# The beginning of a first attention: x of the first batch normalised and turned between two parts of a hidden layer, keys ahead of the other batches' statistics

## The chip, the cores and the metric

The kernel runs on one core of one Trainium2 chip. The metric is the device time of one execution in microseconds; the time of a kernel is the median of its runs. Engine names are those of the profile: PE (TensorE), DVE (VectorE), ACT (ScalarE), POOL (GpSimd), SP (SyncE, which issues the DMAs).

## The reference, cut to what matters

The whole program is two layers, each of an attention with a bias, a second attention, a mixture of experts and a feed-forward block, on x of shape (4, 512, 256). The change touches the first attention's beginning alone. What that attention computes, cut:

```python
xn = ln(x, g_norm)                                # 4 x 512 rows of 256
q = heads(xn @ Wq)                                # 16 heads of 64
k, v = split(xn @ Wkv)                            # one head of 64 for all
k = concatenate([null_kv[0], k]); v = concatenate([null_kv[1], v])
q = l2norm(q) * q_scale;  k = l2norm(k) * k_scale
# the bias: a small network over the positions, one table for all batches
h = silu(ln(pos @ w0 + b0, g0))
h = silu(ln(h @ w1 + b1, g1))                     # the hidden layer
bias = (h @ w2 + b2)[i - j]                       # 16 heads
sim = q k^T * 8 + bias, causal and key mask
out = ln(softmax(sim) v @ Wout, g_out)
```

## The kernel before, in words

`cond_attention` holds five programs, one for each engine, written out in order by hand. An engine takes its instructions in that order and waits on semaphores; `link` makes DVE wait for its own last result. PSUM has eight banks. Banks 0 to 3 hold the small network's results, banks 4 to 7 are a ring (`Ring`): each product of PE takes the next of them with `ring.put`, and waits there until the product four places before it has been emptied by DVE or ACT.

The small network has 640 positions in `NP` = 5 tiles of 128 rows and 256 columns. DVE makes the first hidden rows, ACT applies Silu (`hidden_units`), PE turns them (`turn_hidden`), DVE and ACT copy one half each out of PSUM (`move_hidden`), PE multiplies them by `w1` tile by tile (`hidden_layer`), DVE adds `b1` and takes statistics (`hidden_sums`), aggregates them and adds a constant (`hidden_root`, the TENSOR_SCALAR at L726), ACT takes the Sqrt, DVE normalises (`hidden_rows`), ACT applies Silu, and PE turns the rows again and makes the table (`table`). DVE adds `b2` and SP stores the table to memory and loads it back eight times in its banded form (`cb_toep`), which POOL adds to the masks (L957).

Beside that runs the first batch: four tiles of x, statistics by `row_statistics(0, NT, ...)`, `normalise_x` (L568), `turn_x` on PE into two ring banks (L295), emptied by DVE (bank of c = 0, L573) and ACT (c = 1, L1059), then eight blocks of queries (`queries(0, m)`, PE L329; ACT squares and copies each block, L976 and L977), keys and values (L304), sums of the squared queries over heads (`query_squares`, L337), scores with the null key (`null_scores`, L319), turned keys (L312). DVE normalises the keys (`keys_values`, `scaled_keys`). The null key itself is normalised by `null_key_square`, a Sqrt on ACT and `null_key`; POOL then makes two products of it with Wq (L196), which DVE adds up (`key_sums`, L202). `row_statistics(NT, B * NT, ...)` takes the statistics of the other three batches' x, twelve tiles (L752, L755, L757), which are first used when batch 1 is normalised within the loop of the attention.

The orders before are: PE: turn_hidden(0), the whole hidden layer, both x turns, queries 0, turn_hidden(1), queries 1, table, queries 2 and 3, keys and values, squares, queries 4 to 7, null scores. DVE and ACT: as the left side of the diff shows. The loads are issued by SP in one list at the start (`sync_program`, L1113).

Of the kernel before, what the change touches and what calls it, by code (L numbers as in the profile page):

```python
# [28 lines left out]
NT = S // P  # L29
# [206 lines left out]
def cond_attention(nc, env, w, layer, later=None, gated=None):  # L236
# [8 lines left out]
    with ExitStack() as ctx:  # L245
# [44 lines left out]
        def tensor_program(pe):  # L290
# [144 lines left out]
            def hidden_layer():  # L435
                pe.wait_ge(sm["rp_w"], 16 * 2)
                pe.wait_ge(sm["rp_ev"], 1)
                pe.wait_ge(sm["rp_ev2"], 1)
                for t in range(NP):
# [26 lines left out]
            if L0:  # L466
                turn_hidden(0)
                hidden_layer()
                turn_x(0, 0)
                turn_x(0, 1)  # L470
                pe.wait_ge(sm["cw_q"], 16 * 2)
                queries(0, 0)
                turn_hidden(1)
                queries(0, 1)
                table()
                queries(0, 2)
# [85 lines left out]
        def vector_program(dve):  # L562
# [210 lines left out]
            if L0:  # L773
# [10 lines left out]
                row_statistics(0, NT, "xs_first")  # L784
                null_key_square()
                move_hidden(0)
# [3 lines left out]
                dve.wait_ge(sm["xs_std"], 1)  # L790
                link(dve.reciprocal(rstd[:, 0:NT], r["xve"][:, 0:NT]))
                normalise_x(0)
# [4 lines left out]
                dve.wait_ge(sm["cw_q"], 16 * 2)  # L797
                turn_x(0, 0)
# [8 lines left out]
                dve.tensor_scalar(r["tab"][:, 512:NPOS], PS[0:H, 1, 0:NPOS - 512], r["b2"], None, ALU.add).then_inc(sm["rp_out"], 1)  # L807
                row_statistics(NT, B * NT, "xs_in")
# [3 lines left out]
                keys_values(0)  # L812
                scaled_keys(0)
                query_squares(0, 0)
                dve.wait_ge(sm["xs_std"], 2)
                link(dve.reciprocal(rstd[:, NT:], r["xve"][:, NT:]))
# [8 lines left out]
                spread(("bc", 0, 1), ("q", 0, 1), 0, 1)  # L825
            else:
# [142 lines left out]
        def scalar_program(act):  # L969
# [78 lines left out]
            if L0:  # L1048
                hidden_root(0)
                hidden_units(0)  # L1050
                move_hidden(0)
                act.wait_ge(sm["xs_var"], 1)
                act.activation(r["xve"][:, 0:NT], r["xve"][:, 0:NT], ACT.Sqrt).then_inc(sm["xs_std"], 1)
                act.wait_ge(sm["cw_sum"], 1)
                act.activation(w["sc"][:, 2:3], w["sc"][:, 1:2], ACT.Sqrt).then_inc(sm["cw_root"], 1)
                hidden_root(1)
                bank = ring.take(act, ("x", 0, 1))
                act.wait_ge(sm["cw_q"], 16 * 2)
                act.activation(xnT(0, 1), PS[:, bank, :], ACT.Copy, scale=w["g_in"][:, 1:2]).then_inc(ring.emptied(("x", 0, 1)), 1)  # L1059
                hidden_units(1)  # L1060
                queries(0, 0)
                move_hidden(1)
                for m in range(1, SET + 1):
                    queries(0, m)
                key_root(0)
# [2665 lines left out]
```

## Time and profile before

| | |
|---|---|
| median of 3 runs | 2887.36 us (2885.25 to 2887.46) |
| profiled execution | 2888.08 us, span 2886.3 us |
| PE, weight loads, DVE, ACT, POOL busy | 93%, 55%, 50%, 36%, 32% of the span |
| mean granted clock of PE | 0.96 |
| instructions | 36961 |

The span is the time between the first and the last instruction of the profiled execution; the device time has a little around it. A busy engine is not the same as an engine that sets the end: PE is busy most of the span, and the question in each stretch is what it waits for when it is not. A row of the timeline has the start in us from the span's start, how long the merged instructions took together, the engine, the line of the kernel, the operation, output and inputs with their shapes, the count, and in brackets how long the engine had stood idle before and what released it. The granted clock is 1.00 at PE's full 2.4 GHz and 0.50 at 1.2 GHz.

### The profile page before, as it was taken

Reading aid. Unit: us, or ns where it says so; the run is one execution under the profiler, and the core shown is the slowest. Engines: PE = TensorE matmul, PEld = TensorE weight load, DVE = VectorE, ACT = ScalarE, POOL = GpSimd, SP = SyncE. Lnnn points to the kernel's source line nnn. Section 1 sums busy time; section 2 is a strip of 40 time slices with the busy share of each in tenths; the row PEclk is TensorE's granted clock in tenths of the full one; section 3 lists DMA queues with packets and bytes.
Section 4 is the critical chain, followed back from the end, with each engine's and each line's share of the span. In section 5 each row is a group of like instructions: output and inputs, shape, how many; then the busy total and the mean of one; then the engine's idle time right before and its main releaser. Section 6 shows DMA issues by size and latency. Waiting matters only on the chain. (4 is left out here: it accounts for less than half of the span.)

```text
span 2886.3 us, 36961 instructions
## 1 busy us (share of the span) xinstructions
PE 2680.2 (93%) x13448; PEld 1575.0 (55%) x13448; DVE 1430.9 (50%) x3211; ACT 1052.6 (36%) x2439; POOL 923.5 (32%) x962
## 2 busy tenths in 40 slices
PE   6999998889999889999999999799999899899987
PEld 3555655433333246847748658555555566445555
DVE  6465564356666343234233233655655478355543
ACT  3667675044444201111111111265666255112211
POOL 3555454167676521202102001475655100000000
PEclk9999999799999889999999999999999899899996
DMA  4000001000000060000000010332333000400000
GB/s 147 1 1 1 1 1 19 1 1 1 1 1 1 1 219 1 1 0 1 0 0 1 0 39 1 98 114 89 109 97 103 1 1 1 135 1 15 15 23 22
DMA packets 87961, 91.37 MB, mean 32 GB/s; under 512 B 20982, under 2 KB 71551, under 8 KB 87656
## 3 DMA queue, kind: packets, MB, share of 16 engines
q1 hardware_dynamic: 87784, 89.02, 9.8%
q8 instruction: 110, 1.80, 0.3%
q14 instruction: 67, 0.55, 0.1%
HBM read 86.86 MB, written 2.14 MB: 31 GB/s over the span
## 5 line engine op out<-in xcount | busy, mean ns | idle before, releaser
L957 POOL TENSOR_TENSOR cb_sc<-cb_toep,cb_mk 128x128 f32<-128x128 f32 (+3 forms) x256 | 215.5, 870 | 214.4 <-ACT cb_pr L999 203.8
L957 POOL TENSOR_TENSOR cb_bias<-cb_bias,cb_mk 128x128 f32<-128x128 f32 (+3 forms) x256 | 213.8, 865 | 163.3 <-DMA cb_bias<-in_fside_16xSxS 163.3
L390 PE MATMUL PS<-ident,cb_pr 128*128 128x128 f32 x1280 | 198.9, 287 | 29.3 <-ACT cb_pr L999 27.7
L1542 DVE TENSOR_REDUCE gb_bmax<-PS 128x16 f32<-128x1024 f32 x128 | 156.4, 1223 | 128.5 <-PE PS L1353 127.5
L390 PEld LDWEIGHTS PS<-ident,cb_pr 128*128 128x128 f32 x1280 | 138.6, 143 | 122.3 <-issue 111.4
L661 DVE CUSTOM_DVE_ANT_0 cb_sc<-PS,cb_sc,cb_sneg 128x128 f32<-128x128 f32 (+3 forms) x256 | 130.6, 557 | 138.5 <-PE PS L379 137.0
L3100 POOL TENSOR_TENSOR eb_S<-ff_h 128x1024 f32<-128x1024 f32 x16 | 37.7, 2355 | 466.8 <-PE PS L2054 466.7
L1353 PE MATMUL PS<-gb_ks,gb_qs 32*128 32x512 f32 x512 | 145.9, 647 | 34.1 <-DVE gb_bmax L1542 26.5
L1006 ACT ACTIVATE cb_pt<-PS 128x128 f32<-128x128 f32 (+3 forms) x448 | 162.4, 409 | 36.6 <-PE PS L390 36.1
L1679 ACT ACTIVATE gb_pt<-PS 128x1024 f32<-128x1024 f32 x128 | 130.7, 1021 | 121.1 <-PE PS L1359 112.2
L661 DVE CUSTOM_DVE_ANT_0 cb_bias<-PS,cb_bias,cb_sneg 128x128 f32<-128x128 f32 (+3 forms) x256 | 129.4, 548 | 91.0 <-PE PS L379 90.0
L2054 PE MATMUL PS<-eb_g,ff_h 128*128 128x256 f32 x768 | 173.6, 379 | 0.0
L402 PE MATMUL PS<-cb_pt,cb_kv 128*64 128x512 f32 (+3 forms) x1024 | 157.7, 451 | 10.8 <-DVE cb_pt L669 8.0
L1742 POOL TENSOR_TENSOR gb_pa<-gb_pa,gb_pt 128x512 f32<-128x512 f32 x128 | 159.7, 1273 | 10.9 <-ACT gb_pt L1679 10.6
L379 PE MATMUL PS<-cb_kT,cb_QT 64*128 64x128 f32 (+3 forms) x768 | 156.6, 485 | 1.3 <-DVE cb_kT L602 0.9
L2054 PEld LDWEIGHTS PS<-eb_g,ff_h 128*128 128x128 f32 x768 | 145.9, 190 | 21.5 <-issue 1.9
L999 ACT ACTIVATE cb_pr<-cb_bias,cb_nm 128x128 f32<-128x128 f32 (+3 forms) x256 | 141.4, 557 | 38.6 <-DVE cb_nm L661 38.3
L1359 PE MATMUL PS<-gb_qs,gb_ks 32*128 32x512 f32 x512 | 149.6, 649 | 2.9 <-ACT gb_pt L1679 2.8
L999 ACT ACTIVATE cb_pr<-cb_sc,cb_nm 128x128 f32<-128x128 f32 (+3 forms) x256 | 141.6, 559 | 22.0 <-DVE cb_nm L661 20.6
L402 PEld LDWEIGHTS PS<-cb_pt,cb_kv 128*64 128x64 f32 x1024 | 76.2, 140 | 113.4 <-issue 99.2
L1742 POOL TENSOR_TENSOR gb_pa<-gb_pt 128x512 f32<-128x512 f32 x64 | 79.8, 1269 | 121.8 <-ACT gb_pt L1679 121.8
L2017 PE MATMUL PS<-eb_yT,ff_w 128*128 128x512 f32 x256 | 111.3, 593 | 0.7 <-issue 0.7
(522 smaller groups left out, 5110.9 us busy)
## 6 DMA issues: line engine op xcount, KB each, us to landing
cb_bias<-in_fside_16xSxS SPq DMA_DIRECT2D x64, 256.0 KB, 2.8
cb_bias<-in_fside_16xSxS SPq DMA_DIRECT2D x64, 192.0 KB, 2.4
ff_h<-in_L_ffn_h_w SPq DMA_DIRECT2D x2, 4096.0 KB, 22.7
cb_bias<-in_fside_16xSxS SPq DMA_DIRECT2D x64, 128.0 KB, 2.2
cb_toep<-rel_table SPq DMA_DIRECT2D x8, 512.0 KB, 8.8
cb_bias<-in_fside_16xSxS SPq DMA_DIRECT2D x64, 64.0 KB, 2.3
eb_M<-in_L_ffn_attention_mask SPq DMA_DIRECT2D x4, 1024.0 KB, 5.3
ff_w<-in_L_ffn_w_w SPq DMA_DIRECT2D x3, 1024.0 KB, 7.8
```

What stands on the lines that cost most here:

```text
L379: ins = pe.matmul(PS[:, 2 * (v % 2) + e, 0:n], QT[b % 2][part, m, t * P:t * P + P], kT[part, b % 2, 0:n], start=True, stop=True, tile_posi ...
L390: ins = pe.transpose(PS[:, bank, j * P:j * P + P], pr[:, v % 2, e, j * P:j * P + P], ident)
L402: ins = pe.matmul(PS[part, bank, j * P:S], kv[:, b % 2, j, DH:2 * DH], pt[:, e, j, j * P:S], start=(j == 0), stop=(j == NT - 1), tile_posi ...
L661: ins = dve.tensor_tensor_reduce(out=biases(v, e), in0=PS[:, 2 * (v % 2) + e, 0:n], in1=biases(v, e), scale=-1.0, scalar=sneg[:, b % 2, t, ...
L957: ins = pool.tensor_tensor(biases(v, e), turned(h, n) if L0 else biases(v, e), mk[:, b % 2, packed(t):packed(t) + n], ALU.add)
L999: ins = act.activation(pr[:, v % 2, e, 0:n], biases(v, e), ACT.Exp, bias=nm[:, b % 2, t, k:k + 1], scale=-1.0, accum_out=rs[:, b % 2, t, k ...
L1006: act.activation(pt[:, e, 0:t + 1, t * P:t * P + P], PS[:, bank, 0:width(t)].rearrange("p (j k) -> p j k", k=P), ACT.Copy).then_inc(ring.e ...
L1353: ins = pe.matmul(PS[:, first_bank(x) + e, :], qs[rows(g), n % 3, t * P:t * P + P], ks[rows(g), n % 3, :], start=True, stop=True, tile_pos ...
L1359: ins = pe.matmul(PS[:, 2 + e, :], ks[rows(g), n % 3, t * P:t * P + P], qs[rows(g), n % 3, :], start=True, stop=True, tile_position=(32 * ...
L1542: dve.tensor_reduce(bmax[:, n % 2, t, g:g + 2, 0:NB], PS[:, bank:bank + 2, :].rearrange("p g (n k) -> p g n k", k=64), AX.X, ALU.max)\
L1742: pool.tensor_tensor(pa[:, n % 2, h, :], before, pt[:, n % 2, h, t, :], ALU.add).then_inc(sm["gt_pc"], 1)
L2054: ins = pe.matmul(PS[:, bank, m * HS:m * HS + HS], lhs[:, k, m * P:m * P + P], rhs[:, k, :], start=(m == k == 0), stop=(m == 1 and k == KH ...
```

## The change

Only orders are changed; no instruction is added and none is left out.

On PE the hidden layer is cut: tiles 0 and 1, then both x turns, then tiles 2 to 4. Two blocks of queries come ahead of turn_hidden(1), block 2 ahead of the table, block 3 behind it.

On DVE `move_hidden(0)`, the reciprocal and `normalise_x(0)` come ahead of `null_key_square` and of the first two tiles' sums, and the copy of the turned x comes ahead of `null_key` and the other sums. After the table, the keys, the copy of the squares and the scaled keys come ahead of the twelve tiles' statistics; the reciprocal of those statistics goes to the end, behind the first two spreads.

On ACT the Sqrt of the first batch's variances comes ahead of `move_hidden(0)`, the copy of the turned x ahead of the second hidden root, two blocks of queries ahead of `move_hidden(1)`, the key root after block 3, and the Sqrt of the twelve tiles' variances after block 7.

```diff
-            def hidden_layer():
-                pe.wait_ge(sm["rp_w"], 16 * 2)
-                pe.wait_ge(sm["rp_ev"], 1)
-                pe.wait_ge(sm["rp_ev2"], 1)
-                for t in range(NP):
+            def hidden_layer(tiles):
+                for t in tiles:
+                    if t == 0:
+                        pe.wait_ge(sm["rp_w"], 16 * 2)
+                        pe.wait_ge(sm["rp_ev"], 1)
+                        pe.wait_ge(sm["rp_ev2"], 1)
...
 (PE)
                 turn_hidden(0)
-                hidden_layer()
+                hidden_layer((0, 1))
                 turn_x(0, 0)
                 turn_x(0, 1)
+                hidden_layer((2, 3, 4))
                 pe.wait_ge(sm["cw_q"], 16 * 2)
                 queries(0, 0)
+                queries(0, 1)
                 turn_hidden(1)
-                queries(0, 1)
+                queries(0, 2)
                 table()
-                queries(0, 2)
                 queries(0, 3)
 (DVE)
                 row_statistics(0, NT, "xs_first")
+                move_hidden(0)
+                dve.wait_ge(sm["xs_std"], 1)
+                link(dve.reciprocal(rstd[:, 0:NT], r["xve"][:, 0:NT]))
+                normalise_x(0)
                 null_key_square()
-                move_hidden(0)
                 dve.wait_ge(sm["rp_w"], 16 * 2)
                 hidden_sums(0)
                 hidden_sums(1)
-                dve.wait_ge(sm["xs_std"], 1)
-                link(dve.reciprocal(rstd[:, 0:NT], r["xve"][:, 0:NT]))
-                normalise_x(0)
+                dve.wait_ge(sm["cw_q"], 16 * 2)
+                turn_x(0, 0)
                 null_key()
                 for t in range(2, NP):
                     hidden_sums(t)
                 hidden_root(1)
-                dve.wait_ge(sm["cw_q"], 16 * 2)
-                turn_x(0, 0)
                 hidden_rows(1)
...
+                keys_values(0)
+                query_squares(0, 0)
+                scaled_keys(0)
                 row_statistics(NT, B * NT, "xs_in")
                 dve.wait_ge(sm["ca_zero"], 2)
                 dve.wait_ge(sm["cw_s"], 16 * 5)
                 spread_null_value(dve, w).then_inc(sm["cw_vnb"], 1)
-                keys_values(0)
-                scaled_keys(0)
-                query_squares(0, 0)
-                dve.wait_ge(sm["xs_std"], 2)
-                link(dve.reciprocal(rstd[:, NT:], r["xve"][:, NT:]))
                 null_scores(0)
                 turn_keys(0)
...
                 spread(("bc", 0, 1), ("q", 0, 1), 0, 1)
+                dve.wait_ge(sm["xs_std"], 2)
+                link(dve.reciprocal(rstd[:, NT:], r["xve"][:, NT:]))
 (ACT)
                 hidden_units(0)
-                move_hidden(0)
                 act.wait_ge(sm["xs_var"], 1)
                 act.activation(r["xve"][:, 0:NT], ..., ACT.Sqrt).then_inc(sm["xs_std"], 1)
+                move_hidden(0)
                 act.wait_ge(sm["cw_sum"], 1)
                 act.activation(w["sc"][:, 2:3], w["sc"][:, 1:2], ACT.Sqrt).then_inc(sm["cw_root"], 1)
-                hidden_root(1)
                 (copy of the turned x, c = 1)
+                hidden_root(1)
                 hidden_units(1)
                 queries(0, 0)
+                queries(0, 1)
                 move_hidden(1)
-                for m in range(1, SET + 1):
+                queries(0, 2)
+                queries(0, 3)
+                key_root(0)
+                for m in range(SET, MC):
                     queries(0, m)
-                key_root(0)
                 act.wait_ge(sm["xs_var"], 2)
                 act.activation(r["xve"][:, NT:], ..., ACT.Sqrt).then_inc(sm["xs_std"], 1)
-                for m in range(SET + 1, MC):
-                    queries(0, m)
                 query_roots(0)
```

## Rows read from the trace of the kernel before

**Rows 1.** The chain that ended last (start us, us, what): its oldest long piece

```profile
2474.33 3.15 DMA ex_rows<-in_c_row_of
```

**Rows 2.** Busy time by stretch of PE's clock; the header names the columns

```profile
core 0: us, PE busy (x) PEld busy (x) DVE busy (x) ACT busy (x) POOL busy (x), PEclk, DMA share, GB/s
22.17:25.58 3.41, 0.94 (x8) 0.71 (x7) 3.20 (x14) 0.00 (x0) 2.73 (x2) 1.00 1.05 342
25.58:32.41 6.83, 3.93 (x6) 1.79 (x7) 6.15 (x11) 4.31 (x9) 6.58 (x6) 0.50 0.22 77
32.41:35.82 3.41, 3.41 (x16) 1.68 (x15) 2.01 (x3) 2.24 (x5) 1.15 (x2) 1.00 0.00 0
```

**Rows 3.** The timeline of PE's matmuls, 15 to 57 us

```profile
15.78 6.02 PE L443 MATMUL PS<-cb_pr,cb_pt 128*128 128x256 f32 x20 [1.94 <-DVE cb_pt L739]
22.02 1.10 PE L295 MATMUL PS<-ident,cb_xn 128*128 128x128 f32 x8 [0.22 <-DVE cb_xn L568]
28.48 3.75 PE L329 MATMUL PS<-hTs,ca_wq 128*128 128x512 f32 x4 [5.37 <-ACT hTs L1059]
...
35.12 2.33 PE L453 MATMUL PS<-cb_pt,cb_pr 128*16 128x512 f32 x8
37.38 3.70 PE L329 MATMUL PS<-hTs,ca_wq 128*128 128x512 f32 x8
40.92 1.95 PE L304 MATMUL PS<-ca_wkv,hTs 128*128 128x128 f32 x16
...
43.79 5.42 PE L329 MATMUL PS<-hTs,ca_wq 128*128 128x512 f32 x12
50.75 1.98 PE L329 MATMUL PS<-hTs,ca_wq 128*128 128x512 f32 x4 [1.54 <-DVE cb_nr L622]
52.57 1.85 PE L319 MATMUL PS<-ca_wn,hTs 128*128 128x16 f32 x16
```

**Rows 4.** The timeline of DVE, 13 to 60 us

```profile
17.93 0.42 DVE L743 TENSOR_TENSOR cb_pt<-PS,cb_pt 128x256 f32<-128x256 f32 x1 [2.25 <-PE PS L443]
...
19.25 0.42 DVE L743 TENSOR_TENSOR cb_pt<-PS,cb_pt 128x256 f32<-128x256 f32 x1 [0.43 <-PE PS L443]
...
20.25 1.71 DVE L568 TENSOR_SCALAR cb_xn<-X,cb_mv,cb_rstd 128x256 f32<-128x256 f32 x4
21.88 0.14 DVE L768 TENSOR_SCALAR ca_sc<-ca_sc 128x1 f32<-128x1 f32 x1
...
25.65 1.87 DVE L726 TENSOR_SCALAR cb_pr<-cb_pr 128x5 f32<-128x5 f32 x1
27.43 0.74 DVE L573 TENSOR_SCALAR hTs<-PS,ca_g_in 128x512 f32<-128x512 f32 x1
...
28.30 2.31 DVE L733 SCALAR_TENSOR_TENSOR cb_pt<-cb_pt,cb_pr 128x256 f32<-128x256 f32 x5
...
56.14 0.69 DVE L625 TENSOR_TENSOR cb_nr<-cb_nr,PS 128x512 f32<-128x512 f32 x1 [0.43 <-PE PS L337]
```

**Rows 5.** The timeline of POOL, 20 to 30 us

```profile
21.36 0.46 POOL L926 TENSOR_TENSOR cb_mk<-cb_mk,causal 128x128 f32<-128x128 f32 x1
22.85 4.64 POOL L196 TENSOR_TENSOR cb_QT<-ca_wq,ca_kn 128x1024 f32<-128x1024 f32 x2 [1.04 <-DVE ca_kn L771]
```

**Rows 6.** The timeline of ACT, 13 to 36 us

```profile
13.87 0.70 ACT L1045 ACTIVATE cb_pt<-PS 128x640 f32<-128x640 f32 x1 [0.95 <-PE PS L432]
14.59 1.28 ACT L1053 ACT_TABLE_LOAD   x1
15.89 0.21 ACT L1053 ACTIVATE cb_pr<-cb_pr 128x4 f32<-128x4 f32 x1
...
29.65 2.10 ACT L1040 ACTIVATE cb_pt<-cb_pt,cb_pr 128x256 f32<-128x256 f32 x5
32.27 0.60 ACT L976 ACTIVATE cb_sq<-PS 128x512 f32<-128x512 f32 x1 [0.52 <-PE PS L329]
```

**Rows 7.** DVE's busy time alone: statistics with spread_null_value, keys to reciprocal

```profile
core 0: us, DVE busy (x), PEclk, DMA share, GB/s
38.40:43.96 5.56, 5.47 (x30) 1.00 0.53 133
43.97:50.90 6.93, 4.11 (x10) 1.00 1.04 367
```

## The prediction, made before the changed kernel had run

> **What bounds the kernel now.** I read the page first: PE is busy for 93% of the span. The chain that ended last is almost all PE, but it is followed back only to 2474.33 us [rows 1], so it says nothing of the beginning. After the first attention the profile shows no load that is issued at a fixed time: the later ones are released by the work itself. So I take it that a microsecond saved before the attention's first scores is a microsecond at the end, and read the first 57 us by themselves.
>
> The table of three views, by stretches of PE's clock, shows where PE has nothing to do: in 22.17 to 25.58 it is busy 0.94 us, in the next 6.83 us 3.93, and the clock is down at 1.2 GHz (granted 0.50) from 25.58 to 32.41 [rows 2]. The timeline of PE says why. The first hidden layer runs from 15.78, x is turned at 22.02, and then PE stands 5.37 us until 28.48 for ACT's copy of the turned x [rows 3]. DVE and ACT came to that copy late: DVE normalised x only at 20.25, after two tiles' sums, and copied the turned x at 27.43, after all sums and after a small TENSOR_SCALAR of 128x5 (hidden_root(1)) that took 1.87 us from 25.65 [rows 4]. POOL's two key products run from 22.85 to 27.49 [rows 5]; the small operation ended 0.03 later. From 28.48 PE is nearly full up to 52.57, but for 1.54 us before 50.75, when the query block 7 waits until DVE has emptied the bank of the squares [rows 3]. So the beginning has two holes, and the end of it is the row of null scores at 52.57, behind which keys, squares, norms and spreads follow step by step.
>
> **Part by part. 1: the layer's start.** null_key_square leaves DVE's path ahead of its copy, and ACT puts its Sqrt of the variances ahead of its copy. ACT is free at 12.92 (13.87 less 0.95 idle). Table load 1.28, Sqrt 0.21, copy 0.70 [rows 6]: from 12.93 to about 15.05; DVE's own copy of the same size starts at 13.87 and ends some 0.4 before that. The layer starts at about 15.15 and no longer at 15.78: 0.6 gained. The rows show load and Sqrt with no pause between them (14.59 + 1.28, then 15.89).
> A page speaks against this reorder: the Trainium skill, "ScalarE: Activation LUTs", section "What ACT_TABLE_LOAD costs", gives a table switch a further drain of about 1380 ns beside the load. By that the layer would start 1.4 us later than I say; the trace doesn't show that pause.
>
> **2: x between the tiles.** DVE gets the root at 14.5, normalises in 1.71 as at 20.25 [rows 4] and is through at 16.5; null_key_square (below 0.9, it filled the gap ahead of the old copy) ends at 17.3. Tile 0's sum came 2.15 after the layer's start and tile 1's 3.47 [rows 3, 4]: 17.3 and 18.6 to 18.9 now (the old second tile was partly faster than the first). PE turns x behind tile 1, 18.7 to 19.9 (1.10), so the wait for ca_xn at 16.5 costs nothing. Tiles 2 to 4 follow to about 22.5. DVE's next operation stood 0.8 behind the second sum (the reciprocal ahead of 20.25), so its copy of x is at 19.4 to 19.7 and ends by 20.4; ACT's copy at 19.9 to 20.6. PE can start the queries at 22.5, right behind the layer, where it now waits to 28.48.
>
> **3: hidden layer's root.** Queued behind the x copy on DVE: null_key, three sums, the aggregation, then the small TENSOR_SCALAR. It stood 3.77 behind null_key's first operation (21.88 to 25.65) [rows 4]: 20.1 to 20.4 + 3.77 = 23.9 to 24.2. POOL's masks end at 21.82 as before and hold the products back, since null_key is done by 21.3: products 21.87 to 26.5, the second from 24.2 [rows 5]. Which comes first is within 0.2 us. I take the dearer: the small operation waits as it did and ends at 26.5. ACT then has Sqrt 0.21, load 1.28, and five units of 2.10 [rows 6], with no x copy between: 28.06 to 30.16, where they ended at 31.75. DVE's five products (2.31 at 28.30) start at 27 behind POOL's next cast and keep ahead of ACT.
>
> **4: queries ahead of the table.** PE has two query blocks from 22.5 to 26.1 (1.77 each by 37.38 to 40.92 [rows 3]) and turns the hidden rows as they come, to about 31.0. New wait: ACT's copy of the turned rows now stands behind both blocks' evacuation, four pieces of 0.60 with small overlaps [rows 6], about 2.0: 30.1 to 32.1, copy to 32.8. PE meanwhile runs block 2 from 30.8. The new hole of PE (26.1 to 28.4, then thin turns) will bring the clock down, as after 23.12. If it is at 1.2 GHz until 32.4, block 2 ends at 33.3. The table starts at 33.3, before it was 35.12: **1.8 us**.
>
> **5: from the table to the null scores.** Before: table 2.26, two blocks 3.54, keys and squares 2.87, three blocks 5.42, idle 1.54, the last block 1.82 [rows 3]: 17.45. One of the blocks now lies ahead of the table: **1.8 us**. DVE empties the squares' bank ahead of scaled_keys and the statistics, so block 7 doesn't wait: the 1.54 and the 0.26 in which the block before it drained, **1.8 us**. The rest is 13.9, and the null scores start at 47.2, before it was 52.57.
>
> **6: the statistics of the other batches.** They are moved, not removed: with spread_null_value DVE is busy 5.47 us for them [rows 7]. They now stand behind keys, squares and scaled keys (4.11 with the reciprocal [rows 7]), so the null scores' negation, kT's copy and the sum of squares queue behind them. Keys reach DVE at 39.4. 39.4 + 3.9 + 5.6 = 48.9, plus the wait for the keys' root (0.1 to 0.3), plus what POOL's bias additions cost DVE operations with two SBUF inputs (0 to 0.8): 49.0 to 50.0. The sum of squares at 56.14 [rows 4] stood 3.57 behind the null scores' start: 50.8 now, with some 0.9 of DVE work before it. So DVE has 0 to 0.9 to spare: cost nothing to 0.15; I take nothing. The Sqrt for these statistics moves on ACT behind block 7, at which ACT waits for PE anyhow. The reciprocal of 128x12 (about 0.2) moves behind the second spread, where DVE waits for scores; nothing, and 0.25 if that gap is gone.
> No DMA is added or moved. The table reaches SP 1.8 earlier, so its store and the eight loads too; POOL's first additions are needed only with the first scores.
>
> **Sum:** 1.8 + 1.8 + 1.8 = 5.4 us. The profiled execution took 2888.08 (span 2886.3, 1.8 around it), 0.7 above the median; 2888.08 - 5.4 = 2882.7 for it, and 2887.36 - 5.4 = **2882.0** by the median.
>
> **Rivals.** *The small operation slips in* (30%). It is issued before 24.2 and goes ahead of the second product. Then the root comes 2.1 earlier; but the five products read two SBUF tensors and meet the second product and the cast, so the units end 0.35 to 1.1 earlier, the table too. Gain 5.75 to 6.5, **2881.3**. For it: the estimate's middle lies at the very start of the product. Against: one late DMA of the masks or a slower tile decides it.
> The Trainium skill, "SBUF — State Buffer", section "Who interferes with whom", makes it an exclusive lock: a TENSOR_SCALAR in a two-port mode blocks for GpSimd's whole instruction, and so does an operation with two SBUF inputs while GpSimd reads SBUF. The 1.87 us row agrees. By that rule the five products would gain no more than the cast's end lets them.
> *PE stays slow longer* (13%). If PE's work after the gap keeps 1.2 GHz until 35.8 instead of 32.4, block 2 ends at 34.1 and the table counts as begun at 35.0: gain 3.7, **2883.7**. Against: full work from 28.99 brought 2.4 GHz back at 32.41 [rows 2]; now that stretch is less full.
> *DVE's statistics become the bound* (6%): POOL additions blocking more than I allow, or the keys later; 1 to 2 us lost behind them, **2883.5**.
> *ACT's reorder costs a pause* (2%): the change of function ahead of the copy takes a second 1.28 [rows 6] in its new place; layer and x are that much later, of which 0.4 is slack ahead of POOL's products: gain 4.5, **2882.9**. This is the page's rule of step 1 as this kernel would show it.
> *It does not reach the end* (3%): the attention's loop takes the time back; about **2887**.
> *Slower* (2%): PE stays at 1.2 GHz for all 13.9 us of step 5, so these take 27.8, and the table is late as above: 10 us lost in place of 5.4 won, **2898**. It decides from 10.8 us of PE-bound work at the lower clock beyond what I count: then the gain is gone.
> The rest (44%) is the forecast.
>
> **How the numbers follow.** What this kernel's measurement can tell from no change is about 0.2%, 5.8 us: below 2881.6 is faster. The forecast's own range is 2880.5 to 2883.3 (0.6 for the table's start, 0.4 for DVE in step 6, 0.7 for how PE's clock falls on the attention's first scores; the three runs before lay 2.2 apart): a third of it is below 2881.6. With two thirds of the first rival: 0.15 + 0.19 + 0.03 from scatter = 0.37 faster. Slower 0.04, same 0.59. The range takes in both upper cases and the lower: 2879.3 to 2885.3.
>
> **What would show it.** Right: the layer at 15.1 to 15.3; x turned at 18.7 on PE, between tiles; queries behind it at 22.5 without idle; the small operation ending at 26.5 (or at 24.4: the rival); table at 33.3; no idle before block 7; null scores at 47.2; the sum of squares 3.6 behind it. Wrong: the null negation much later than 2 us behind its matmuls (DVE bound), a granted clock of 0.5 after 32.4, or a start that is 5 us earlier and an end that is not.

## The result and the profile after

The changed kernel takes 2881.24 us (median of 15 runs, 2873.75 to 2886.85); the kernel before, run beside it, 2887.46 (15 runs, 2881.88 to 2893.81). The ratio is 0.9979, 95% interval 0.9969 to 0.9989: 6.2 us less, between 3 and 9. A later measurement of the same pair on another occasion (12 and 23 runs) gave 0.9975 (0.9964 to 0.9987). The forecast was 2882.0. Both intervals leave 1 out, so the gain is clear of the noise, and small.

The profiled execution has a span of 2879.5 us, against 2886.3; its device time is 2881.24. PE is busy 2680.1 us (2680.2 before) and the mean granted clock is 0.96 in both: what went is PE's idle time.

PE's matmuls from the hidden layer to the sum of squares, the timeline of the changed kernel (columns as in the rows of before; L444 is the hidden layer, before L443, L454 the table, before L453). To be laid beside [rows 3]:

```profile
15.09 3.75 PE L444 MATMUL PS<-cb_pr,cb_pt 128*128 128x256 f32 x8 [1.34 <-ACT cb_pt L1047]
18.64 1.09 PE L295 MATMUL PS<-ident,cb_xn 128*128 128x128 f32 x8
19.56 2.76 PE L444 MATMUL PS<-cb_pr,cb_pt 128*128 128x256 f32 x12
22.15 3.60 PE L329 MATMUL PS<-hTs,ca_wq 128*128 128x512 f32 x8
28.51 2.34 PE L432 MATMUL PS<-ident,cb_pt 128*128 128x128 f32 x10 [2.76 <-ACT cb_pt L1042]
30.64 2.75 PE L329 MATMUL PS<-hTs,ca_wq 128*128 128x512 f32 x4
33.32 2.33 PE L454 MATMUL PS<-cb_pt,cb_pr 128*16 128x512 f32 x8
...
40.27 7.13 PE L329 MATMUL PS<-hTs,ca_wq 128*128 128x512 f32 x16
47.24 1.85 PE L319 MATMUL PS<-ca_wn,hTs 128*128 128x16 f32 x16
```

The wait of 5.37 us ahead of the queries is gone, and so is the 1.54 ahead of block 7: sixteen instructions, four blocks, now stand in one piece. One wait is new, 2.76 ahead of the turn of the hidden rows. The table starts at 33.32 instead of 35.12, the null scores at 47.24 instead of 52.57: 5.33 us.

How far one execution can be trusted shows in the other profiles of the same two kernels (r_before, r_after, after_again). From the table to the null scores it is 17.45 and 17.44 us in the two of the kernel before, 13.92, 13.93 and 13.92 in the three of the changed one: these 3.5 us are there every time. The start of the table moves about: 35.12 and 34.81 before, 33.32, 33.50 and 34.11 after. So the null scores come 4.2 to 5.3 us earlier, whichever two executions are compared.

DVE in the same execution (L728 is the second hidden root, before L726; L735 the five products, before L733; L610 negates the null scores, L627 sums the squares, before L625; L827 is the reciprocal of 128x12):

```profile
24.11 2.28 DVE L728 TENSOR_SCALAR cb_pr<-cb_pr 128x5 f32<-128x5 f32 x1
...
26.89 2.57 DVE L735 SCALAR_TENSOR_TENSOR cb_pt<-cb_pt,cb_pr 128x256 f32<-128x256 f32 x5
...
49.14 0.22 DVE L610 TENSOR_SCALAR cb_sneg<-PS 128x64 f32<-128x64 f32 x1 [0.53 <-PE PS L319]
49.69 0.69 DVE L604 COPY cb_kT<-PS 128x512 f32<-128x512 f32 x1 [0.33 <-PE PS L312]
50.81 0.69 DVE L627 TENSOR_TENSOR cb_nr<-cb_nr,PS 128x512 f32<-128x512 f32 x1 [0.43 <-PE PS L337]
...
58.37 0.22 DVE L827 RECIPROCAL cb_rstd<-cb_pr 128x12 f32<-128x12 f32 x1
```

DVE still waits for PE at all three of its steps behind the null scores' matmuls (0.53, 0.33 and 0.43 us idle), so the statistics that now stand ahead of them do not set the end. The sum of squares is 5.33 us earlier as well.

The two profiles' spans differ by 6.8 us, but this is not 5.3 us kept and 1.5 added for good. Followed through the program, the distance between the two executions goes up and down behind the beginning. The first product with the values (L402 in both) starts at 78.31 before and 71.48 after, 6.8 apart; the second attention's output product at 2464.36 and 2460.49, 3.9 apart; the next turn of x at 2472.16 and 2465.75, 6.4 apart. The timelines of PE at that last place, first the kernel before, then the changed one:

```profile
2464.36 6.24 PE L3317 MATMUL PS<-cc_wo,cd_OT 128*128 128x256 f32 x16 [0.88 <-DVE cd_OT L3454]
2472.16 1.06 PE L1940 MATMUL PS<-ident,X 128*128 128x128 f32 x8 [1.56 <-PEq L3569]
```

```profile
2460.49 3.69 PE L3320 MATMUL PS<-cc_wo,cd_OT 128*128 128x256 f32 x16 [1.03 <-DVE cd_OT L3457]
2465.75 1.06 PE L1943 MATMUL PS<-ident,X 128*128 128x128 f32 x8 [1.56 <-PEq L3572]
```

The same sixteen instructions take 6.24 us in one and 3.69 in the other, and the granted clock of that stretch (the table by stretches, columns as in [rows 2], before and then after) is 0.66 in one and 1.00 in the other:

```profile
2462.00:2472.00 10.00, 7.63 (x24) 5.79 (x24) 2.76 (x4) 0.00 (x0) 0.00 (x0) 0.66 0.01 2
```

```profile
2455.00:2465.00 10.00, 6.61 (x54) 4.87 (x43) 3.77 (x7) 0.60 (x1) 0.00 (x0) 1.00 0.01 2
```

Nothing of the change lies there: these 2.55 us are the clock's, and they account for the step from 3.9 to 6.4. What took the distance from 6.8 down to 3.9 in between was not looked for. The clock also goes with the time of whole runs: over 23 runs of the kernel before, the mean granted clock lies between 0.957 and 0.964 and the time between 2892.19 us (at 0.957) and 2879.48 (at 0.964), with a correlation of -0.93. The runs of one kernel spread over 12 to 13 us, and the ratio's interval is 6 us wide. The beginning itself is read from the traces.

### The profile page after: what moved, and what is told of

The parts are those of the page before. It is cut to its first block and busy times, and to the rows that moved or that the text cites. A ratio compares the mean times of both kernels' runs of the same rounds, so it can differ in the third digit from the quotient of the medians.

```text
span 2879.5 us, 36960 instructions
## 1 busy us (share of the span) xinstructions
PE 2680.1 (93%) x13448; PEld 1574.2 (55%) x13448; DVE 1430.6 (50%) x3211; ACT 1052.5 (37%) x2439; POOL 923.2 (32%) x962
## 5 line engine op out<-in xcount | busy, mean ns | idle before, releaser
L390 PE MATMUL PS<-ident,cb_pr 128*128 128x128 f32 x1280 | 198.1, 286 | 29.5 <-ACT cb_pr L1001 27.8
L402 PE MATMUL PS<-cb_pt,cb_kv 128*64 128x512 f32 (+3 forms) x1024 | 158.0, 451 | 10.3 <-DVE cb_pt L671 7.8
L402 PEld LDWEIGHTS PS<-cb_pt,cb_kv 128*64 128x64 f32 x1024 | 76.2, 140 | 112.9 <-issue 98.1
## 6 DMA issues: line engine op xcount, KB each, us to landing
ff_h<-in_L_ffn_h_w SPq DMA_DIRECT2D x2, 4096.0 KB, 23.7
```

What stands on the lines that cost most here:

```text
L390: ins = pe.transpose(PS[:, bank, j * P:j * P + P], pr[:, v % 2, e, j * P:j * P + P], ident)
L402: ins = pe.matmul(PS[part, bank, j * P:S], kv[:, b % 2, j, DH:2 * DH], pt[:, e, j, j * P:S], start=(j == 0), stop=(j == NT - 1), tile_posi ...
```

## The experiments

Of the two halves, each was made alone. The front half ends with the table; the back half is what DVE and ACT do behind it. Five of the experiments, and two repeats, have a single run each, which is also the profiled one: e1_front 2891.18 us, e2_back 2890.72, e4_stats_twice 2888.27, e6_x_only 2886.08, e5_fill 2883.07, and the repeats r_before 2887.50 and r_after 2881.72. Against a spread of 12 us in the runs of one kernel these times decide nothing, so the experiments are read from their traces.

**The front half alone** (e1_front). The changed kernel, with this taken back on DVE and the old order of squares and roots on ACT to match:

```diff
-                keys_values(0)
-                query_squares(0, 0)
-                scaled_keys(0)
                 row_statistics(NT, B * NT, "xs_in")
                 spread_null_value(dve, w).then_inc(sm["cw_vnb"], 1)
+                keys_values(0)
+                scaled_keys(0)
+                query_squares(0, 0)
+                dve.wait_ge(sm["xs_std"], 2)
+                link(dve.reciprocal(rstd[:, NT:], r["xve"][:, NT:]))
```

> The changed kernel with its back half undone: after the table, DVE and ACT have their old orders (statistics of twelve tiles ahead of keys, scaled keys ahead of the copy of the squares). My theory: the table still starts at 33.3 us, but the statistics hold the keys until 42.2, the key root and the squares' copy end near 47.4, and query block 7 waits for that copy about 2 us: null scores at 49.1 to 49.6, 3.2 us before the 52.57 of the kernel before, where the whole change gained 5.3. Rival: PE's order alone carries the gain, DVE's order behind the table is hidden: no idle before block 7, null scores at 47.2.

Measured: table at 33.18, keys on DVE at 42.05, null scores at 51.20, 1.4 us earlier than in [rows 3] and not 3.2. PE and then DVE:

```profile
48.37 3.04 PE L329 MATMUL PS<-hTs,ca_wq 128*128 128x512 f32 x4 [2.81 <-DVE cb_nr L624]
51.20 3.44 PE L319 MATMUL PS<-ca_wn,hTs 128*128 128x16 f32 x16
```

```profile
45.27 0.96 DVE L595 TENSOR_TENSOR cb_xn<-cb_kv,cb_ks 128x256 f32<-128x256 f32 x1
46.27 1.44 DVE L598 TENSOR_TENSOR cb_kd<-cb_xn,ca_qr 128x256 f32<-128x256 f32 x2
47.63 0.68 DVE L624 COPY cb_nr<-PS 128x512 f32<-128x512 f32 x1
```

The rival is out: the back half is needed. What I had too small is the size: the wait is 2.81, since the three products of the keys take 2.40 where the changed kernel's took 1.19 (0.43 and 0.76; POOL's bias additions, from 42.58 to 47.09, run beside them here), and behind the wait the clock is down, so that block 7 takes 3.04 and not 1.98. It stays at 0.50 up to 69.6, and the null scores' own matmuls take 3.44 in place of 1.85. The first product with the values starts at 80.67, 2.4 us later than in the first profile of the kernel before. So in this one execution the half that moves PE's work forward gained 1.4 us up to the null scores and had lost it again at the values. That it loses every time is not shown, since the clock's low stretches fall differently from one execution to the next.

**The back half alone** (e2_back): the kernel before with DVE's keys, squares and scaled keys ahead of the statistics, the reciprocal behind the second spread, and ACT's order to match.

> The kernel before with only the back half of the change (keys, squares and scaled keys ahead of the statistics on DVE, the matching order on ACT). My theory: the table starts at 35.1 as before, block 7 no longer waits, null scores at 50.8, 1.8 us earlier; the sum of squares 3.6 behind them, at 54.4. Rival: the moved statistics bound what follows, and the sum of squares stands at 55 or later, so that the half alone gives under 1 us.

Measured, PE and then DVE:

```profile
36.71 2.33 PE L453 MATMUL PS<-cb_pt,cb_pr 128*16 128x512 f32 x8
...
52.35 1.85 PE L319 MATMUL PS<-ca_wn,hTs 128*128 128x16 f32 x16
```

```profile
47.94 1.97 DVE L596 TENSOR_TENSOR cb_kd<-cb_xn,ca_qr 128x256 f32<-128x256 f32 x2
...
56.40 0.69 DVE L625 TENSOR_TENSOR cb_nr<-cb_nr,PS 128x512 f32<-128x512 f32 x1
```

Block 7 doesn't wait. The null scores start 15.64 behind the table (forecast 15.7, before 17.45), so the term is there, 1.8 us. By the absolute times the forecast missed: null scores at 52.35 and not 50.8, the sum of squares at 56.40 and not 54.4, which is no earlier than in the kernel before (56.14). There are two reasons. The table is 1.6 late in this execution. 0.6 of that is there when the queries start (29.10 in place of 28.48); the layer starts at 16.18 and takes 7.11 us in place of 6.02, at a granted clock that reads 1.00 in both, so this part is not put down to the clock here. The rest lies in the ten turns (2.34 in place of 1.45) and the block behind them, where the clock is at 0.50 up to 35.0. The second reason is DVE: the sum of squares stands 4.05 behind the null scores and not 3.57, with no idle of DVE ahead of it. The statistics do bind here, by 0.5 us. POOL's bias additions start at 46.07, ahead of the scaled keys, whose three products then take 0.69 and 1.97 us, where the changed kernel's took 0.43 and 0.76. So theory and rival were both partly right.

**Statistics twice** (e4_stats_twice): the changed kernel, and the loop of twelve bn_stats again in front of the aggregation.

> The changed kernel with the twelve tiles' statistics taken twice (4.0 us more DVE work at their new place). My theory: DVE has only 0.5 us to spare there and 0.7 us further on, so the negation of the null scores moves from 49.1 to 52.7 and the sum of squares from 50.8 to 53.6, 2.8 us later; null scores' matmuls themselves stay at 47.2. Rival: there is much more room there than I think and the sum of squares moves by less than 1 us.

Measured, DVE of that kernel:

```profile
47.15 4.02 DVE L758 BATCH_NORM_STATS2 cb_pr<-X 128x6 f32<-128x256 f32 x12
...
52.74 0.22 DVE L610 TENSOR_SCALAR cb_sneg<-PS 128x64 f32<-128x64 f32 x1
53.00 0.69 DVE L604 COPY cb_kT<-PS 128x512 f32<-128x512 f32 x1
53.72 0.69 DVE L627 TENSOR_TENSOR cb_nr<-cb_nr,PS 128x512 f32<-128x512 f32 x1
```

The negation starts at 52.74 (expected 52.7), the sum of squares at 53.72 (53.6), the null scores at 47.30. The 4.05 us added came out as 2.9: DVE had 1.1 to 1.2 us to spare in all, out of the three idles of the changed kernel (0.53, 0.33 and 0.43).

**x between the tiles, queries where they were** (e6_x_only): the changed kernel with

```diff
                 queries(0, 0)
-                queries(0, 1)
                 turn_hidden(1)
-                queries(0, 2)
+                queries(0, 1)
                 table()
+                queries(0, 2)
                 queries(0, 3)
```

> The changed kernel with PE's order of the queries taken back (block 0, turn of the hidden rows, block 1, table, blocks 2 and 3; ACT's order to match); x between the tiles stays, and so does the back half. My theory: the x part and the query part are separate terms of 1.8 us each. The table starts at 33.3 to 34.2 (block 1 at the lower clock ahead of it, the hole of PE being longer), and one block more stands behind it: null scores at 49.0 to 49.9, 1.8 to 2.7 us later than the 47.2 of the whole change. Rival: x between the tiles alone brings everything, since the root and Silu of the hidden rows set the table: null scores within 0.5 us of 47.2.

Measured:

```profile
34.20 2.33 PE L454 MATMUL PS<-cb_pt,cb_pr 128*16 128x512 f32 x8
...
49.84 1.85 PE L319 MATMUL PS<-ca_wn,hTs 128*128 128x16 f32 x16
```

The null scores come 2.6 us later than with the whole change. The rival is out. Of the 2.6, 1.72 is the block behind the table (15.64 from the table to the null scores, in place of 13.92) and 0.88 the table's start, behind a hole of 4.08 us on PE. The start alone is not sure, since it came at 33.50 and 34.11 in other executions of the changed kernel. The other way round, with x turned behind the whole layer and the queries moved, nothing was run, nor was ACT's reorder ahead of the layer by itself: what these two bring is read from the changed kernel's rows. DVE showed something that I had priced at 0 to 0.8 us:

```profile
44.10 0.73 DVE L593 TENSOR_SCALAR cb_ks<-cb_ks 128x4 f32<-128x4 f32 x1
44.86 0.18 DVE L594 RECIPROCAL cb_ks<-cb_ks 128x4 f32<-128x4 f32 x1
45.08 0.69 DVE L595 TENSOR_TENSOR cb_xn<-cb_kv,cb_ks 128x256 f32<-128x256 f32 x1
45.80 2.25 DVE L598 TENSOR_TENSOR cb_kd<-cb_xn,ca_qr 128x256 f32<-128x256 f32 x2
```

POOL's additions started at 43.25 here, ahead of the scaled keys. In the changed kernel the scaled keys ended at 43.13 and POOL started at 43.14, and the same operations took 0.16, 0.43 and 0.76. Here they take 2.3 us more, and the sum of squares starts 4.70 behind the null scores, bound by DVE, where 3.57 is PE's own distance. The same was seen in e2_back. In all three profiles of the changed kernel the key products took 0.43 and 0.76, but with next to nothing to spare: the additions start at 43.14, 43.04 and 43.99, the products end at 43.13, 43.31 and 43.92. That the whole change pays nothing for it depends on whether the loaded table arrives before or after the scaled keys.

**The small operation and POOL's products** (e3_products). In the changed kernel, POOL waits for the second hidden rows before its two products, and DVE copies the turned rows ahead of its first key sum:

```diff
                 pool.wait_ge(sm["cw_q"], 16 * 2)
+                pool.wait_ge(sm["rp_norm"], 2 * NP)
                 for c in range(DC):
                     key_products(...)
...
-                dve.wait_ge(sm["cw_prod"], 1)
-                key_sums(dve, w, r["prod0"], 0)
                 move_hidden(1)
+                dve.wait_ge(sm["cw_prod"], 1)
+                key_sums(dve, w, r["prod0"], 0)
```

> The changed kernel, but POOL's two key products wait until DVE has normalised the second hidden rows, and DVE copies the turned rows ahead of its first key sum. My theory: the small TENSOR_SCALAR of the second hidden root is held by POOL's product; without it it takes 0.17 us instead of 2.28, ends at 24.3, Silu runs 25.9 to 28.0, the table starts at 30.7 instead of 33.3 and the null scores at 44.6 instead of 47.2: 2878.6 by the changed kernel's 2881.2, 0.3 percent under the kernel before. Rival: the small operation is slow by itself or for another engine (1.9 to 2.3 us again), the table stays at 33.3. Second rival: the products, now later, hold the null scores' weights back: key sums end after 44.6 and the gain is gone.

Measured, by the timelines of DVE and PE:

```profile
24.46 0.17 DVE L728 TENSOR_SCALAR cb_pr<-cb_pr 128x5 f32<-128x5 f32 x1
24.91 0.19 DVE L732 RECIPROCAL cb_pr<-cb_pr 128x5 f32<-128x5 f32 x1 [0.27 <-ACT cb_pr L1038]
25.13 2.07 DVE L735 SCALAR_TENSOR_TENSOR cb_pt<-cb_pt,cb_pr 128x256 f32<-128x256 f32 x5
```

```profile
30.96 2.31 PE L454 MATMUL PS<-cb_pt,cb_pr 128*16 128x512 f32 x8 [0.46 <-ACT cb_pt L1048]
...
44.87 1.85 PE L319 MATMUL PS<-ca_wn,hTs 128*128 128x16 f32 x16
```

0.17 us in place of 2.28, table at 30.96 (30.7 expected), null scores at 44.87 (44.6): 2.4 earlier than the changed kernel. Both rivals are out. The time was 2873.51 us (9 runs), ratio to the kernel before 0.9962 (0.9947 to 0.9978): 11 us, which is more than the traces' 7.7 us at the null scores.

So it was measured again, with the changed kernel beside it on one chip (e3_again and after_again):

> The kernel with the late products once more, beside the changed kernel on one chip. By the traces its null scores come 2.4 us earlier than the changed kernel's and 7.7 earlier than those of the kernel before: 2.4 us below the changed kernel, ratio to before 0.9973. If the first measurement (0.9962) was no scatter, something behind the beginning gains too, and the ratio is 0.996 again.

> The changed kernel once more: ratio to before 0.9979 to 0.9982 (5.3 us in 2887, by the traces' null scores), null scores at 47.2 to 47.5 in its profile.

Measured: e3_again 2880.48 (12 runs), ratio 0.9976 (0.9965 to 0.9987), null scores at 44.49; after_again 2878.85 (12 runs), 0.9975 (0.9964 to 0.9987), null scores at 48.03. The first 0.9962 did not come again; the intervals overlap, and it is taken as scatter. For after_again I had expected the null scores at 47.2 to 47.5, and they came at 48.03: its layer starts at 15.75 in place of 15.09, its table at 34.11. In the two pairs of executions the late products' null scores stand 2.4 and 3.5 us earlier; by the total time the two kernels can't be told apart.

**The clock in the new hole** (e5_fill): the changed kernel with query block 1 multiplied twice into one bank; the first pass is overwritten, so the result is that of the changed kernel with 1.7 us more of PE work.

> The changed kernel with query block 1 multiplied twice into the same bank (its first pass is thrown away), so that PE has 1.7 us more to do in the hole ahead of the turn of the hidden rows (25.8 to 28.5 in the changed kernel's profile). My theory: PE's clock is not taken down in the stretch behind the hole; turn and block 2 run at 2.4 GHz, block 2 is through at 32.4, and the table starts when ACT's copy of the turned rows ends, at 32.7 in place of 33.3; null scores at 46.6: the added work makes the start 0.6 us earlier. Rival: what the clock does there isn't set by that hole, block 2 still takes 2.75 us, table at 33.3 and null scores at 47.2.

Measured:

```profile
30.51 1.88 PE L330 MATMUL PS<-hTs,ca_wq 128*128 128x512 f32 x4
32.86 2.31 PE L455 MATMUL PS<-cb_pt,cb_pr 128*16 128x512 f32 x8 [0.46 <-ACT cb_pt L1048]
...
46.77 1.85 PE L319 MATMUL PS<-ca_wn,hTs 128*128 128x16 f32 x16
```

Block 2 takes 1.88 in place of 2.75 and the table waits for ACT's copy, as I had expected, though it is 0.46 us earlier and not 0.6. Table and null scores both come that much earlier. (ACT's copy ends at 32.71 here and at 32.57 in the changed kernel, so 0.1 of the 0.6 went there.) In the changed kernel, the stretches of the clock read (columns as in [rows 2]):

```profile
22.00:25.50 3.50, 3.50 (x10) 1.46 (x8) 3.36 (x11) 0.00 (x0) 3.50 (x2) 1.00 1.04 344
25.50:28.91 3.41, 0.65 (x4) 0.21 (x3) 3.10 (x6) 2.46 (x5) 3.33 (x4) 1.00 0.51 175
28.91:32.33 3.42, 3.42 (x11) 2.06 (x11) 3.18 (x7) 3.42 (x8) 3.17 (x4) 0.51 0.00 0
```

PE is idle for most of the second, and at 1.2 GHz in the third, while it works. With the hole filled, the second and third read:

```profile
25.50:28.91 3.41, 3.10 (x9) 1.15 (x7) 3.10 (x6) 2.32 (x5) 3.33 (x4) 1.00 0.56 196
28.91:32.33 3.42, 3.42 (x14) 1.45 (x12) 3.42 (x7) 3.42 (x9) 3.17 (x4) 1.00 0.01 4
```

The clock stays up, and the rival is out: adding work to the hole made the kernel's start faster. It is not a gain in the total: the first product with the values starts at 72.51 in this execution, 1.0 later than in the changed kernel's first profile, for a reason that the table further down shows.

**The clock behind the null scores** (e7_busy, e8_busy_small). Behind the null scores PE waits three times for DVE and ACT, and then makes the two spreads (L358). Into these waits of the kernel with the late products went eight matmuls whose result nobody reads, two, three and three: with 512 columns in e7_busy, with 256 in e8_busy_small.

```diff
                 query_squares(0, 1)
+                keep_busy(2)
                 turn_squares(0)
+                keep_busy(3)
                 turn_rows(("rn", 0), 1)
+                keep_busy(3)
                 pe.wait_ge(sm["cw_sel"], 2)
```

> The kernel with the late products (e3_products) and eight thrown-away matmuls of 512 columns, two, three and three, in PE's three waits behind the sums of squares (1.1, 1.7 and 1.7 us), 3.4 us of work in idle time. My theory: PE's clock is not taken down at 50.7, where the kernel without them ran 13.7 us at 1.2 GHz; the null scores stay at 44.9, the two spreads go from 1.19 to 0.8 us, and the attention's first values start 23.0 to 23.7 us behind the null scores, not 24.7: 1.0 to 1.7 earlier. Rival: DVE and ACT set that stretch, PE's clock costs nothing there, and the distance stays within 0.3 us of 24.7. Second rival: the added matmuls don't fit into the waits and delay what follows them. The total should then be 1 to 2 us below the 2873.5 of that kernel, which 15 runs a side can't tell.

> The kernel with the late products and the eight thrown-away matmuls, now with 256 columns (0.43 us each, 0.9, 1.3 and 1.3 us in waits of 1.1, 1.7 and 1.7); with 512 columns each took 0.86 and overran the waits by 1.1 us in all. My theory: PE stays at 2.4 GHz from 50.7 on and nothing is delayed: spreads start 9.6 us behind the null scores as without them, and the attention's first values 23.6 to 24.0 behind, in place of 24.7. Rival: the clock is worth nothing here and the distance is 24.7 again. By the total, 1 us can't be told.

Measured, e7_busy: the clock does stay up from 44 to 70 us, but I had priced a matmul at half: each takes two instructions of 0.43, and the spreads start 10.7 us behind the null scores, not 9.6. The first values come 24.9 behind, where I expected 23.0 to 23.7. By that number alone either rival could stand. The parts decide for the second: 1.1 lost up to the spreads, and 0.95 won from there to the next turn of x (10.31 in place of 11.26). So the clock is worth something, and the added work took it again. The time was 2881.09 us (7 runs), ratio 0.9969 (0.9958 to 0.998), where I expected 1 to 2 us below 2873.5.

e8_busy_small: the spreads take 0.70 us in place of 1.19 and nothing is delayed (9.1 behind). The first values come 24.5 behind, where I expected 23.6 to 24.0 and the rival 24.7. The stretches show why:

```profile
50.70:65.40 14.70, 10.35 (x58) 6.22 (x59) 12.92 (x38) 7.00 (x25) 4.91 (x6) 1.00 0.00 1
65.40:68.80 3.40, 3.40 (x16) 2.58 (x15) 2.42 (x8) 2.82 (x11) 3.29 (x4) 0.50 0.00 0
```

The clock was kept up to 65.4 and fell there instead, behind another wait of PE (2.35 us from 62.2, for DVE). Up to the turn of x behind that wait, 1.7 us had been won (19.1 us from the null scores in place of 20.8 in e3_products); the low stretch then took 1.5. Why the clock fell there and not in e7_busy, which has the same wait (2.33 us) and the same turns behind it, the traces don't show. The time was 2872.65 us (6 runs), ratio 0.9954 (0.9937 to 0.9971). The intervals of this kernel, the one with the late products and the changed one overlap, and in its profile the first values start at 69.89, where the one with the late products had 69.58 and 70.24. That it is the fastest is not shown.

**Both kernels profiled once more** (r_before, r_after).

> The kernel before, profiled once more. If PE's clock, whose stretches fall differently from one execution to the next, is what makes the time behind the beginning differ by several microseconds, the null scores stand at 52.6 within 1.7 us and the span differs from 2886.3 by up to 5 us, in places where the granted clock of the two executions differs. If the profiled execution was typical, all of it repeats within 1 us.

> The changed kernel, profiled once more. My theory: null scores at 47.2 within 1 us and the sum of squares 3.6 behind; the small TENSOR_SCALAR of the second hidden root either takes over 2 us or under 0.4, and in the second case the five products behind it take 4.7 us, so that the table starts at 33.2 to 33.4 either way. Span 2872 to 2885, the difference from the first profile lying where the granted clocks differ. Rival: without the wait of the small operation the table starts 0.4 us or more earlier, as I had forecast.

Measured: r_before has the null scores at 52.25, the sum of squares 3.56 behind, span 2885.7; r_after 47.43, 3.56 and 2879.9. In r_after the small operation takes 0.17:

```profile
24.08 0.17 DVE L728 TENSOR_SCALAR cb_pr<-cb_pr 128x5 f32<-128x5 f32 x1
24.75 4.64 DVE L735 SCALAR_TENSOR_TENSOR cb_pt<-cb_pt,cb_pr 128x256 f32<-128x256 f32 x5
```

and the five products behind it 4.64; the table starts at 33.50. So the rival is out: without the wait of the small operation the table came no earlier. In r_before the null scores stand 0.3 us from those of the first profile and the span 0.6, but the first values 1.5 (76.78 and 78.31): not all of it repeats within 1 us, and where it doesn't, the granted clocks differ.

From the null scores to the first values the executions show this. The last column is the last part of that way, from the turn of the second batch's x (L295) to the first product with the values (L402):

| kernel | clock down from (us long) | first values behind null scores | from the turn of x on |
|---|---|---|---|
| changed | 56.3 (6.8) | 24.2 | 3.86 |
| changed, r_after | 53.4 (10.2) | 24.7 | 3.86 |
| changed, after_again | 54.2 (10.2) | 24.7 | 3.86 |
| before, r_before | 59.1 (10.2) | 24.5 | 3.86 |
| late products | 50.7 (13.7) | 24.7 | 3.87 |
| before | 59.7 (6.8) and 73.4 (3.4) | 25.7 | 5.33 |
| late products, e3_again | 52.3 (6.8) and 66.0 (3.4) | 25.8 | 5.35 |
| changed, e5_fill | 54.6 (6.8) and 68.3 (3.4) | 25.7 | 5.35 |

Where a second low stretch falls on the turns ahead of the first values, 1.5 us are lost there; this is in three of the eight, one of each kind of kernel. The profiled execution of the kernel before had it and that of the changed kernel had not. That is the 1.5 us by which the two profiles differ more at 78 us than at 52. A longer first low stretch goes with 0.3 to 0.5 us more up to the turn of x (20.67 to 20.86 us from the null scores, in place of 20.4).

## Why the prediction was right

The time (2881.24 for 2882.0) and the sum (5.4) stand; the null scores were forecast at 47.2 and are at 47.24, the sum of squares at 50.8 and is at 50.81. That these agree to some hundredths is in part the luck of which execution was profiled: in r_after the null scores are at 47.43 and in after_again at 48.03, and the kernel before had them at 52.25 in r_before. What repeats is the mechanism, and the 3.5 us of its last two terms to 0.01. By the steps:

1. *The layer's start.* Forecast 15.15, is 15.09 (15.48 and 15.78 in the two profiles of the kernel before, 15.06 and 15.75 in the repeats of the changed one). ACT's rows in the new place:

```profile
12.86 1.28 ACT L1054 ACT_TABLE_LOAD   x1
14.15 0.21 ACT L1054 ACTIVATE cb_pr<-cb_pr 128x4 f32<-128x4 f32 x1
```

ACT's Silu ends at 12.84, so there is no pause ahead of the load or behind it, and the rival that rested on a pause did not show. The Trainium skill ("ScalarE: Activation LUTs", "What ACT_TABLE_LOAD costs") adds a drain to each switch of the table; the trace doesn't agree with it here.
2. *x between the tiles.* Turned at 18.64 (18.7), queries at 22.15 (22.5), without idle.
3. *The second hidden root.* Issued at 24.11, within the 23.9 to 24.2 that I gave, and it waited, as I had taken. That which of two comes first is open was right as well: in r_after, e1_front and e4_stats_twice it took 0.17 to 0.32, in the changed kernel's profile, e5_fill, e6_x_only and after_again 1.89 to 2.28. What was wrong is the price of the rival. I gave it 0.35 to 1.1 us; it gains 0.1, or nothing: table at 33.18, 33.38 and 33.50 with it, 33.32 without. Either the small operation waits for POOL's second product, or the first of the five products behind it does (4.64 to 4.66 for the five, not 2.1), and the rows are through at 29.4 to 29.5 in both. So the step costs the same whichever of the two comes first. The Trainium skill's rule ("SBUF — State Buffer", "Who interferes with whom") names both forms; the trace agrees, with one exception: POOL's TENSOR_SCALAR on the masks (1.57 us from 28.99 in the profile before, also reading SBUF) did not hold DVE's products there, five of which took 2.31 [rows 4], against 2.07 with nothing beside them in e3_products. Only e3_products, which takes POOL's products away from both, gains, 2.4 us.
4. *Queries ahead of the table.* Clock down from 28.9 to 32.4, block 2 through at 33.3, table at 33.32: as written. What the lower clock costs in it is 0.46 us, by e5_fill.
5. *From the table to the null scores.* 13.92 for 13.9. The term of the block and the term of the wait are real: without the first, in e6_x_only, this stretch takes 15.64, and with the second alone, in e2_back, 15.64 as well, where the kernel before has 17.45. They don't stand alone: e1_front shows 1.4 where the first two terms together are 3.6, for without the back half the wait grows from 1.54 to 2.81 and block 7 behind it runs at the lower clock (3.04 in place of 1.98).
6. *The statistics.* Taken as nothing, and it was nothing; DVE had 1.1 us to spare (e4_stats_twice), where I gave it 0 to 0.9. My bound of 0.8 for POOL's additions was too small: 2.3 in e6_x_only, 1.7 in e2_back. Had the table arrived a microsecond or two sooner in the changed kernel, the rival in which DVE sets the end could have come true. I had not worked out which comes first, and that it came out well is in part luck.

The range of 2879.3 to 2885.3 holds the median of 15 runs, but not every single run (2873.75 to 2886.85), and on the later occasion the changed kernel's median was 2878.85, 0.45 below it, with the kernel before at 2886.09. What the range left out is scatter of the whole program, more than of the beginning. I gave a chance of 0.59 to a time that can't be told from no change and 0.37 to a faster one, with a limit of 5.8 us between them. With 15 runs a side the interval is 6 us wide in all and lies wholly on one side of no change, and 6.2 us is beyond my limit as well: the size was right, and the less likely of the two outcomes came. Whether all of the 5.3 us reaches the end was not tested by itself; the total agrees with it (3 to 9 us for 5.3), no more.

## What to carry to other kernels

When an engine is full but for two holes, a reorder is priced by writing the new start of each step from the durations of the old trace. Over 30 us that held to 0.1 us in one execution here and to 0.2 and 0.8 in two others. Two halves of such a reorder need not be worth their share alone: the half that only moves the wait gained 1.4 us of its 3.6 at the null scores. When an operation is held by another engine, it does nothing to move it forward if the next one of the held kind takes its place; look at which operation of the other engine holds it, and move that.

## What the runs showed of the hardware

- POOL's product of two SBUF inputs (2.3 us) held a DVE TENSOR_SCALAR of 128x5 for up to 2.28 us, or a product with two SBUF inputs, whichever was issued into it; with POOL's products elsewhere they took 0.17 and 0.41. bn_stats and operations that read PSUM ran beside it at their usual time (0.43 and 0.41). POOL's additions of two SBUF inputs held the three key products in the same way: 2.9 us in e6_x_only and 2.7 in e2_back, in place of 1.2.
- PE's clock fell to 1.2 GHz in or behind waits of PE (2.8 us and 5.4 us ahead of the table, 2.1 to 2.4 ahead of the turn of the second x) and cost 0.46 us in one place and 1.5 in another. It did not fall behind every wait: 1.55 us ahead of that turn brought nothing in the changed kernel. Work that nobody needs, put into the waits, kept it at 2.4 GHz (e5_fill, e7_busy, e8_busy_small). In e8_busy_small the fall came 15 us later instead, behind a wait of 2.35 us; in e7_busy, with the same wait, it didn't come at all.
- In the hidden layer of the changed kernel the first eight matmuls took 3.75 us and the next twelve 2.76, while the granted clock reads 1.00 for both. So in the first 20 us of these traces a pace of half speed stands beside a granted clock of 1.00.
- The two profiled executions were 3.9 to 6.8 us apart along their way. At two places, of 1.5 and 2.5 us, it is shown that the clock fell in one and not in the other. So a profile of one execution each says nothing about a difference of 1 us far from its cause.
